# Attention-weighted products of a graph layer: two operations of four tiles instead of four of two

## The reference

```python
Wh = (h @ W.T + b).reshape(N, HEADS, HEAD_DIM)
e = leaky_relu(alpha_src[idx_i] + alpha_dst[idx_j], 0.2)
ex = exp(e - m[idx_i])
denom = segment_sum(ex, idx_i)
out = segment_sum((ex / denom[idx_i])[:, :, None] * Wh[idx_j], idx_i)
```

## Time and profile before

| | us |
|---|---|
| median of 3 runs | 3190.27 (3189.21 to 3194.09) |
| the profiled execution | 3205.1 |
| its span, first to last instruction | 3203.4 |
| GpSimd busy | 2163.3 |
| TensorE busy | 2181.0 |
| VectorE busy | 1919.5 |
| ScalarE busy | 753.7 |

### The profile page before, as it was taken

One profiled execution on the slowest core, in us unless ns is written; L12 is line 12 of the kernel. 1 busy time (PEld: TensorE's weight loads), 2 busy tenths in 40 slices (PEclk: granted clock), 3 DMA queues, 4 the chain that ended last, 5 costly groups with the idle time before them and its releaser, 6 DMA issues.

```text
span 3203.4 us, 40657 instructions
## 1 busy us (share of the span) xinstructions
PE 2181.0 (68%) x10817; PEld 1528.2 (48%) x10818; DVE 1919.5 (60%) x3954; ACT 753.7 (24%) x1346; POOL 2163.3 (68%) x2140
## 2 busy tenths in 40 slices
PE   0000687037778868787787978878768787787877
PEld 0000454025555555555555655555555555555554
DVE  8999554036565574656666465575654655756563
ACT  0000343012322222222222222222212222222222
POOL 0003777667777777777777777777777777777770
PEclk6555899568898998888889989898989888899988
DMA  5000122143434444444444434434444344344463
GB/s 183 0 0 1 54 72 66 18 118 91 116 92 105 121 102 123 100 110 113 103 122 101 121 103 104 124 101 123 102 105 123 98 111 117 99 124 102 122 93 31
DMA packets 271533, 305.63 MB, mean 95 GB/s; under 512 B 164258, under 2 KB 210856, under 8 KB 271080
## 3 DMA queue, kind: packets, MB, share of 16 engines
q0 software_dynamic: 97760, 251.60, 30.3%
q1 hardware_dynamic: 140098, 18.08, 3.8%
q10 hardware_dynamic: 33480, 33.36, 3.2%
HBM read 276.25 MB, written 26.62 MB: 95 GB/s over the span
## 4 chain that ended last, share of the span: by engine, by line
PE 34%; POOL 23%; issue 11%; DVE 9%; ACT 1%; DMA 1%; POOLq 0%; DVEq 0%; SPq 0%; ACTq 0%
POOL gathered L933 23%; PE sum_banks L1007 18%; PE f_banks L1022 7%; DVE onehot L1410 3%; PE turned L979 2%; PE f_banks L1066 1%; PE f_banks L1141 1%; DVE gathered L1431 1%; PE sum_banks L995 1%; DMA gathered<-table,col 1%; PE f_banks L1047 1%; PE f_banks L1142 1%; PE f_banks L1048 1%; DVE he L1559 1%; DVE he L1562 1%
## 5 line engine op out<-in xcount | busy, mean ns | idle before, releaser
L933 POOL DMA_INDIRECT gathered<-table,col x1872 | 1904.7, 1017 | 594.7 <-issue 564.5
L1007 PE MATMUL sum_banks<-gathered,onehot 128*128 128x260 f32 x3744 | 1060.8, 445 | 103.2 <-DVE gathered L1431 102.5
L1007 PEld LDWEIGHTS sum_banks<-gathered,onehot 128*128 128x128 f32 x3744 | 818.0, 224 | 292.2 <-issue 129.9
L1431 DVE TENSOR_TENSOR gathered<-gathered 128x512 f32<-128x512 f32 x936 | 591.5, 692 | 46.5 <-ACT gathered L1186 43.7
L1410 DVE TENSOR_TENSOR onehot<-iota_row,col 128x1024 f32<-128x1024 f32 x236 | 288.8, 1224 | 476.0 <-PE sum_banks L1007 447.9
L283 POOL DMA_INDIRECT edge_list<-payload,pos x244 | 247.1, 1013 | 349.9 <-DVE pos L400 273.0
L1182 ACT COPY onehot_t<-turned 128x1024 bf16<-128x1024 bf16 x236 | 238.7, 1011 | 398.0 <-PE turned L979 392.0
L1196 ACT COPY acc<-sum_banks x234 | 88.0, 376 | 870.3 <-PE sum_banks L1007 721.2
L979 PE MATMUL turned<-ident_bf,onehot 128*128 128x128 bf16 x1888 | 158.4, 231 | 188.9 <-DVE onehot L1410 188.8
L979 PEld LDWEIGHTS turned<-ident_bf,onehot 128*128 128x128 bf16 x1888 | 116.1, 103 | 207.0 <-DVE onehot L1410 168.9
L989 PE MATMUL scores<-t,onehot_t 128*128 x1880 | 102.2, 175 | 141.8 <-DVE scored L1419 98.8
(11 more groups left out here) (316 smaller groups left out, 2499.8 us busy)
## 6 DMA issues: line engine op xcount, KB each, us to landing
gathered<-table,col POOLq DMA_INDIRECT x1872
xn_batch<-xn ACTq DMA_DIRECT2D x13, 512.0 KB, 4.4
x_all<-in_x SPq DMA_DIRECT2D x1, 6144.0 KB
x_batch<-in_x ACTq DMA_DIRECT2D x12, 512.0 KB
out<-xf ACTq DMA_DIRECT2D x12, 512.0 KB
edge_list<-xn_all SPq DMA_DIRECT2D x2, 2176.0 KB, 13.7
edge_list<-payload,pos POOLq DMA_INDIRECT x244
col<-edge_list SPq DMA_DIRECT2D x236, 8.0 KB, 2.1
```

What stands on the lines that cost most here:

```text
L933: g.indirect_dma_start(gathered[:, l, t, :], None, sh["table"], bass.IndirectOffsetOnAxis(ap=col[l][:, t // G, t % G, 0:1], axis=0)).then_ ...
L1007: last = t.matmul(sum_banks[:, ds(banks_of[g], 1), 0:TB].rearrange("p a w -> p (a w)"), onehot[:, l % 3, g * G + k, :], gathered[:, l, g * ...
L1431: v.tensor_tensor(value, value, gathered[:, l, tiles, C:TB].unsqueeze(3).broadcast_to([P, G, H, HD]), ALU.mult).then_inc(s_mul, 1)
```

## The change

`product` now covers half a lot, four tiles (128x1024), and is called twice for a lot instead of four times. TensorE's `sums` waits before the first and the third group instead of before each, for a semaphore that now counts two products to a lot. The values computed, the gathers, the onehots, the matrix products and their order are as before.

```diff
@@ sums (TensorE)
                 for g in range(GROUPS):
-                    pe.wait_ge(s_mul, n * GROUPS + (g + 1))
+                    if g % 2 == 0:
+                        pe.wait_ge(s_mul, n * 2 + (g // 2 + 1))
                     for k in range(G):
@@ product and lot (VectorE)
-            def product(it, l, g):
-
-                tiles = slice(g * G, g * G + G)
+            def product(it, l, half):
+
+                some = TILES // 2
+                tiles = slice(half * some, half * some + some)
                 value = gathered[:, l, tiles, 0:C].rearrange("p k (a d) -> p k a d", d=HD)
-                v.tensor_tensor(value, value, gathered[:, l, tiles, C:TB].unsqueeze(3).broadcast_to([P, G, H, HD]),
+                v.tensor_tensor(value, value, gathered[:, l, tiles, C:TB].unsqueeze(3).broadcast_to([P, some, H, HD]),
                                 ALU.mult).then_inc(s_mul, 1)
...
-                for g in range(GROUPS):
-                    product(it, l, g)
+                for half in range(2):
+                    product(it, l, half)
```

## The result

| | before | changed |
|---|---|---|
| median, us | 3191.26 (3189.21 to 3194.09) | 3343.83 (3340.86 to 3345.45) |
| ratio | | 1.0476 (1.0458 to 1.0495) |
| profiled execution, us | 3205.1 | 3345.0 |
| span, us | 3203.4 | 3343.3 |

What follows compares the result with a forecast made beforehand. GpSimd's chain of gathers was taken as the bound from 900 us on. Longer holds +125, later sums +5 and shorter VectorE work -3 made +127 us, 3332 profiled, forecast 3317 us; range 3226 to 3348.

Steps and rivals of the forecast that it cites:

- GpSimd's chain is the bound: From 900 us on, 1688 gathers form one chain; every nanosecond added to a gather is added to the time.
- The rule of the hold: A gather starting over 0.03 us after certain VectorE instructions, 0.13 or more before their end, ends about 0.82 after it.
- the phase set by the onehot: A gather held by the onehot makes the next start 1.20 us after the first product; 81 lots.
- (a): In 114 lots after 900 us the second product newly holds a gather, 1.03 us each: +117 us.
- (b): In 28 lots a gather already held by the first product is held to 1.23 instead of 0.69 us: +15 us.
- (c): Remaining gathers, 0.7 or 1.1 us after the first product, lose a few hundredths each: -3 us.
- The feedback of shifted phases: Shifted gathers meet later onehots in another phase; the gathers' sum of +129 us was taken as +125.
- the replay: The hold rule applied gather by gather over the whole trace, two products against four: +123 us, between 120 and 135.
- the edge: A gather starting 0.03 us after a product is not held; one starting 0.05 us after is.
- The sums' first wait: TensorE gets its first half 0.54 us later: +5 us before 900 us, free after, with slack of 7 us a stretch.
- first and last rivals: First: second product too late to hold, 3230 us, chance 0.12. Last: nothing changes, 3192 us, chance 0.05.
- VectorE's 0.16 us less per lot: Two products take 2.37 us, not 2.53; 37 us over 234 lots, off the path after 900 us, -3 before.

Runs made afterwards that it cites:

- e1: The kernel before, its four products kept, with TensorE waiting only before the first and third group, for the second and fourth product; 3296.2 us.
- e9: The changed kernel, with VectorE waiting for its first product to be complete before issuing the second; 3298.6 us.
- e3: The kernel before, with the onehots made by eight comparisons of one tile against a scalar per partition; 3357.1 us.
- e5: The changed kernel with a memset of 128 columns between the two products of a lot; 3336.4 us.
- e7: The kernel before with four products, TensorE waiting for halves, and 8 more matrix products of zeros in mix slots with that wait; 3231.0 us.
- e6: The changed kernel with a memset of 128 columns between the products and 8 more matrix products of zeros in mix slots; 3336.0 us.
- e8: The kernel before with eight products of one tile (128x256), TensorE waiting before each group for its second product; 3229.8 us.
- e10: The changed kernel with VectorE waiting between the two products and 8 matrix products of zeros in the mix slots; 3217.9 us.

## Why the prediction was right, and where it wasn't

*GpSimd's chain is the bound, and every nanosecond on a gather is on the time.* Right for these two kernels: +149 us of gathers, -8 of waits for sums, +2 of issue, -3 of tail, +140 of time. It was a closer thing than the prediction says, since TensorE's side was just behind (e1). The signs that the prediction named came too: 1097 ns in the mean for 1085, 99 gathers of 1.96 us behind the start of a second product, longer waits of VectorE for landings (161.9 for 86.0 us).

*The rule of the hold and the phase set by the onehot.* Right for two-input instructions that follow each other, the only case that the trace of before showed. e9 shows the decisive part, that these holds are what GpSimd's chain paid: with a wait and 0.11 us between the products the 99 holds are gone. The rule fails behind the comparisons by scalar and the memset (e3, e5).

*Term (a), 114 x 1.03 = 117 us.* Measured 99 gathers at 1.02, 100.8 us. *Terms (b) and (c), +12.* Measured: the rest of the products' holds grew from 24.6 to 47.8, +23. Products together +124, where the sum had +129.

*The feedback of shifted phases, put at -4 by the replay.* Wrong: lines 1590 and 1470 crossed the edge (+24.4), the onehots took 8 more, line 1562 6 less. That is +26 where the sum had -4, 30 us of error. The forecast is only 13 off, 127 for 140, because other terms erred the other way: products 5, GpSimd's shorter waits 8, tail 3. That part is luck. The gathers that start within 0.01 us of an instruction could be read from the trace; I left these two lines out of the replay because they held nothing.

*The sums' first wait, free after 900 us.* This step failed. I priced the wait and not what comes with it, TensorE's lower clock: 10 us in the stretch read and not 2, against a slack that was no 7 us there but none; 103 us by itself (e1), 62 of them given back by the filler (e7). In the changed kernel it stayed hidden, as GpSimd's chain had grown by more (e5 and e6, with the same holds, are alike; the filler alone was not put into the changed kernel). The forecast came out right since the two costs don't add: the longer of two chains counts. Had the holds been absent, as in my first and last rivals, the time would have been 3300 and not 3230 or 3192. In that sense their prices were wrong by 70 to 100 us.

*VectorE's 0.16 us less per lot is worth nothing.* Right: 39 us less of product time, no gain.

## What to carry to other kernels

Before VectorE work is packed into fewer, longer instructions, see in the timeline whether gathers issued by GpSimd end a fixed time after them; here a gather waited for the end of the instruction it met, so the longer products cost more than they saved, and a few hundredths of a microsecond of phase decided how often. Shorter isn't better of itself either: eight products cost 40 us (e8). When a wait on TensorE is made longer, price the lower clock behind it too, by the same products in rows at either clock. And when one chain is the bound, measure the next one by making only its part of the change: undoing one cause of two showed 43 us of 153 (e9), undoing the other none (e6 against e5), undoing both 124 (e10).

## What the runs showed of the hardware that I had not expected

- A gather that met back-to-back two-input instructions right behind a comparison by scalar was mostly let in only after the last of the four (2.89 us instead of 0.95; 83 of 107 in e3, none of 25 where VectorE had idled between); behind a memset it was held by an instruction that started 0.07 us after it (2.04 us).
- In the pair of lots shown, with 0.6 us more of idle time on TensorE ahead of the sums, the granted clock was 0.66 instead of 0.80 in the next lot, and its 16 products took 6.72 instead of 4.96 us. Products of zeros in the idle time took e1 from 3296 to 3231 us.
- A memset of one column between two products (0.06 us in the trace) moved the second by about 0.01 us only.
